# Two four-image tiles become eight one-image units in a diffusion and deformable-convolution kernel

## The chip, the cores and the metric

The kernel runs on one core of a Trainium2 chip. The metric is the device time of one execution in microseconds. The core has a matrix engine (PE, with its weight loads shown apart as PEld), a vector engine (DVE), an activation engine (ACT), GpSimd (POOL) and a sync engine that issues DMAs (SP). Each works through its own instruction list in order and waits on semaphores.

## The reference

`x` is `(8, 32, 32, 64)` in float32 (image, row, column, channel). Two residual layers, each behind a group normalization with groups of two channels, act on it. The first is five steps of a diffusion whose coefficients come from gradients and two depthwise 3x3 convolutions; the second is a deformable 3x3 convolution that samples nine displaced points per pixel bilinearly.

```python
g, g1 = relu(bn(dwconv(h, wg))), relu(bn(dwconv(h, wg1)))
gy, gx = sobel(h)
Dx, Dy = 1 / (gy*gy/4 + 1), 1 / (gx*gx/4 + 1)
...
for _ in range(5):
    prev = h
    h = D * (c0*h0 - 2*E*h + cm_x*roll(h, 1, 2) + cp_x*roll(h, -1, 2)
             + cm_y*roll(h, 1, 3) + cp_y*roll(h, -1, 3)) + D * 0.4 * fsrc
    h0 = prev
...
o1, o2, m = split(conv3x3(x, w_offset) + b_offset)   # 9 + 9 + 9 channels
sampled = bilinear(x, base_y + o1, base_x + o2) * sigmoid(m)   # 9 taps, 64 channels
out = einsum('bkcp,fck->bfp', sampled, filt)
```

## The kernel before

128 partitions hold the 32 rows of four images. There are two tiles (`TILES`) of four images; a tile's free dimension is 32 columns by 64 channels, 2048 numbers per partition (`WC`). Each tile goes through normalization, gradients, depthwise convolution, coefficients, 20 diffusion chunks of 512 numbers (`pde 0` to `pde 19`), the second normalization and the offsets. Then its 32 image columns are sampled one by one.

The sampling of a column works so. SP has written the normalized tile into a table in HBM, in which one entry of 1 KB holds the four corner pixels of a bilinear sample. POOL issues nine gathers per column (L378), one for each tap, each of 128 rows by 1 KB. DVE multiplies the gathered corners by their weights (L748), adds them in two steps (L755, L761), PE transposes the sums in five 128x128 pieces (L1056), ACT copies them to SBUF (L921), and PE multiplies with the filter (L1064, five products with 64 columns). A group of four columns is added to `x1` (L730) and stored (L356). `pixels` has room for four columns.

The order of the work on DVE, ACT and PE is one list written out by hand (`SCHEDULE`, turned into `ORDER`): tile 0 up to its first column, then tile 1's pieces with tile 0's columns between them, then tile 1's columns alone. In the second and third part the table of tile 1 is written and POOL goes on from tile 0's 288 gathers to tile 1's 288. SP first issues the loads, then eight DMAs that clear the table (L338), then per tile eight that fill it (L351).

In the diffusion PE sums five products per chunk by multiplying them with the identity (L1037); DVE forms the products (L576, L580, L586), both operands in SBUF, and adds the kept rest (L597). In the profile one call of `matmul` on float32 is two MATMUL records; one `transpose` is one record.

## Time and profile before

| | |
|---|---|
| time, median of 3 runs | 1076.55 us (1072.9 to 1078.05) |
| the profiled execution | 1075.92 us, its span 1074.0 us |
| busy: PE, PEld | 612.7 us (57%), 399.3 us (37%) |
| busy: DVE, ACT | 673.2 us (63%), 214.5 us (20%) |
| busy: POOL | 628.6 us (59%), of it 626.3 us in 576 gathers |
| first and last gather start | 251.7 and 1058.0 us |
| mean granted clock of PE | 0.727 of 2.4 GHz |

Busy time is what the instructions of an engine cover. Two matmuls in a row overlap in the records, so what one costs in a stream is the distance between starts. DMA-issuing time of SP is not counted as busy.

### The profile page before, as it was taken

The numbers are of one execution on the slowest core, as the hardware profiler recorded it, in microseconds if no ns is written. First come the engines' busy times: TensorE is split into PE (matmuls) and PEld (weight loads), VectorE is DVE, ScalarE is ACT, GpSimd is POOL, SyncE is SP. The second block draws the span as 40 slices with busy tenths as digits, with TensorE's granted clock in tenths as the row PEclk, the third lists the DMA queues.
The fourth block names the chain that finished last, engine by engine and source line by source line (L and its number), as shares of the span: only waits on it lengthen the run. The fifth ranks groups of instructions, "written<-read, shape, count | busy, mean of one in ns | idle before, by whom it ended". The sixth has DMA issues, their size and how long they took to land.

```text
span 1074.0 us, 7428 instructions
## 1 busy us (share of the span) xinstructions
PE 612.7 (57%) x2314; PEld 399.3 (37%) x2314; DVE 673.2 (63%) x685; ACT 214.5 (20%) x577; POOL 628.6 (59%) x588
## 2 busy tenths in 40 slices
PE   1987999468985678958843667523222322322233
PEld 1773434123775244434323433323222322322233
DVE  6799999843788676858887446543344334334433
ACT  2721000022523223133213411200000000000000
POOL 0000000004888777877787777777777777777773
PEclk9998999779987878987975686655555555555555
DMA  6431000054222233233222583333333333333331
GB/s 217 132 120 43 0 0 1 0 110 111 84 74 74 79 93 93 77 87 95 85 83 88 133 254 105 93 106 103 107 99 105 107 97 107 101 107 98 106 107 56
DMA packets 58144, 100.35 MB, mean 93 GB/s; under 512 B 10168, under 2 KB 39040, under 8 KB 57856
## 3 DMA queue, kind: packets, MB, share of 16 engines
q0 software_dynamic: 27648, 75.53, 23.8%
q1 hardware_dynamic: 30464, 24.42, 8.4%
q8 instruction: 17, 0.28, 0.1%
q14 instruction: 15, 0.12, 0.0%
HBM read 79.13 MB, written 20.78 MB: 93 GB/s over the span
## 4 chain that ended last, share of the span: by engine, by line
POOL 58%; issue 20%; DVE 12%; PE 5%; ACT 2%; DMA 2%; SPq 1%; POOLq 0%; DVEq 0%
POOL pixels L378 57%; PE acc L1037 3%; DVE rsum L434 2%; SPq L351 1%; DVE shared L586 1%; DVE shared L576 1%; DMA table<-scratch 1%; DVE h_pad L597 1%; DVE shared L556 1%; DVE shared L580 1%; PE acc L959 1%; DMA x<-x_in 0%; DVE scratch L430 0%; DVE scratch L415 0%; PE acc L1005 0%
## 5 line engine op out<-in xcount | busy, mean ns | idle before, releaser
L378 POOL DMA_INDIRECT pixels<-table,index_now x576 | 626.3, 1087 | 180.2 <-issue 172.4
L748 DVE TENSOR_TENSOR pixels<-pixels,side 128x2304 f32<-128x2304 f32 (+1 forms) x64 | 148.2, 2315 | 260.8 <-DMA pixels<-table,index_now 260.4
L1056 PE MATMUL side<-const,sums 128*128 128x128 f32 x320 | 74.1, 388 | 352.7 <-DVE sums L761 324.4
L1037 PE MATMUL acc<-shared,const 128*128 128x512 f32 x400 | 196.1, 635 | 22.7 <-DVE shared L576 22.7
L1056 PEld LDWEIGHTS side<-const,sums 128*128 128x128 f32 x320 | 53.3, 199 | 369.4 <-issue 239.3
L370 POOL COPY index_now<-index 128x72 uint32 x8 | 2.1, 260 | 250.0 <-DMA table<-scratch 250.0
L921 ACT ACTIVATE sampled_T<-side 128x384 f32<-128x384 f32 (+1 forms) x128 | 49.7, 433 | 403.3 <-PE side L1056 403.2
L1064 PEld LDWEIGHTS side<-filt,sampled_T 128*128 128x128 f32 x640 | 126.3, 296 | 0.0
L1064 PE MATMUL side<-filt,sampled_T 128*128 128x64 f32 x640 | 125.8, 373 | 0.0
L1037 PEld LDWEIGHTS acc<-shared,const 128*128 128x128 f32 x400 | 77.8, 202 | 128.0 <-issue 108.3
L755 DVE TENSOR_TENSOR pixels<-pixels 128x1152 f32<-128x1152 f32 x64 | 86.9, 1358 | 7.4 <-ACT pixels L910 5.4
L910 ACT ACTIVATE pixels<-pixels,corner_w 128x64 f32<-128x64 f32 x228 | 56.5, 334 | 135.6 <-DMA pixels<-table,index_now 135.6
L586 DVE TENSOR_TENSOR shared<-arrays,h_pad 128x1024 f32<-128x1024 f32 x40 | 48.8, 1220 | 7.4 <-PE acc L1037 7.3
L580 DVE TENSOR_TENSOR shared<-arrays,h_pad 128x1024 f32<-128x1024 f32 x40 | 48.7, 1219 | 5.5 <-PE acc L1037 5.5
L761 DVE TENSOR_TENSOR sums<-pixels 128x576 f32<-128x576 f32 x64 | 48.5, 758 | 4.9 <-PE side L1056 0.5
L959 PE MATMUL acc<-conv_w,shared 128*128 128x256 f32 x128 | 39.5, 391 | 4.5 <-DVE h_pad L509 4.5
L576 DVE TENSOR_TENSOR shared<-arrays,h_pad 128x512 f32<-128x512 f32 x40 | 27.5, 688 | 18.4 <-ACT h_pad L800 18.4
L935 PE MATMUL acc<-rsum,const 128*128 128x64 f32 x16 | 4.9, 403 | 54.8 <-DVE rsum L434 54.0
L597 DVE TENSOR_TENSOR h_pad<-acc,shared 128x512 f32<-128x512 f32 x40 | 27.4, 685 | 2.1 <-PE acc L1037 2.1
L556 DVE TENSOR_TENSOR shared<-arrays,h_pad 128x512 f32<-128x512 f32 x40 | 27.6, 690 | 0.9
L1035 PE MATMUL acc<-arrays,const 128*128 128x512 f32 x50 | 25.5, 593 | 0.0
L935 PEld LDWEIGHTS acc<-rsum,const 128*128 128x128 f32 x16 | 3.6, 281 | 57.2 <-DVE rsum L434 55.6
(158 smaller groups left out, 744.0 us busy)
## 6 DMA issues: line engine op xcount, KB each, us to landing
table<-corner_w SPq DMA_DIRECT2D x8, 1225.0 KB
pixels<-table,index_now POOLq DMA_INDIRECT x576, 2.8
table<-scratch SPq DMA_DIRECT2D x16, 528.0 KB, 10.4
x<-x_in SPq DMA_DIRECT2D x2, 1024.0 KB, 7.2
out_dram<-x SPq DMA_DIRECT2D x16, 128.0 KB, 1.9
const<-const_in SPq DMA_DIRECT2D x1, 641.0 KB, 6.0
xn_next<-bn_in SPq DMA_DIRECT2D x1, 384.0 KB, 7.1
off_w<-offw_in SPq DMA_DIRECT2D x1, 288.0 KB, 7.1
```

The lines of the kernel that those rows point to most:

```text
L378: pool.indirect_dma_start(out=pixels[:, w % COLS, k, :], out_offset=None, in_=table, in_offset=bass.IndirectOffsetOnAxis(ap=index_now[:, o ...
L580: dve.tensor_tensor(two(wc(prod[:, prod_slot(n, 1), :]), wc(prod[:, prod_slot(n, 2), :])), two(coef(2), coef("mid")), two(moved(0, -1), mo ...
L586: dve.tensor_tensor(two(wc(prod[:, prod_slot(n, 3), :]), wc(prod[:, prod_slot(n, 4), :])), two(coef(3), coef(0)), two(moved(-1, 0), moved( ...
L748: dve.tensor_tensor(quads[:, 0:cells, :], quads[:, 0:cells, :], weights[:, 0:cells].unsqueeze(2).to_broadcast([P, cells, C]), ALU.mult)\
L755: dve.tensor_tensor(px[:, :, 0:2 * C], px[:, :, 0:2 * C], px[:, :, 2 * C:4 * C], ALU.add)\
L761: dve.tensor_tensor(sums[:, j % 2, 0:K2 * C].rearrange("p (k c) -> p k c", c=C), px[:, :, 0:C], px[:, :, C:2 * C], ALU.add).then_inc(s_sum ...
L910: ins = act.activation(cell, cell, ACT.Copy, scale=corner_w[:, 0, w, 4 * k + q:4 * k + q + 1])
L921: act.activation(sampled_T[:, j % 2, a * P:b * P], turned[:, r, 0:(b - a) * P], ACT.Copy)\
L959: ins = pe.matmul(dst, turned_pair(dh, pair), w3[:, 0:4 * C], start=dh == 0, stop=False)
L1037: pe.matmul(bank(t, "pde", i), eye, prod[:, prod_slot(n, j), :], start=j == 0, stop=j == PRODS - 1)\
L1056: ins = pe.transpose(turned[:, r, (i - a) * P:(i - a + 1) * P], sums[:, j % 2, i * P:(i + 1) * P], eye)
L1064: ins = pe.matmul(out[:, j * C:(j + 1) * C], sampled_T[:, j % 2, k * P:(k + 1) * P], filt[:, k, :], start=k == 0, stop=k == TAP_PAIRS - 1)
```

## The change

A unit is now one image: its 32 columns are split into four sides of 8 columns, and partition `side * 32 + row` holds one side of a row. `WC` becomes 512, one PSUM bank. There are eight units, each with 8 columns per partition to sample, so 64 columns and 576 gathers in all, as before.

- The list of pieces per unit is `BESIDE`: eight parts, and part `w` of unit u+1 stands ahead of column `w` of unit u. The prediction calls part `w` with the column behind it slot `w`. Unit 0's parts stand alone at the start.
- The diffusion's arrays, of 512 numbers per partition, lie in PSUM banks 0 to 3; DVE's large operations then take one operand at least from PSUM. The neighbours across sides come by products with `prev` and `next`, so a step has nine products: four of 448 to 504 columns, one of 512, two of 64 and two of 8. DVE no longer adds the rest, it seeds the target bank.
- Column: DVE only multiplies, into `weighted`. PE adds the four corners while it transposes: for each of five pieces four transposing products accumulate (20 in all, "flips"). Then the filter as before.
- `pixels` has room for seven columns, and POOL takes its indices from `index` without a copy.
- The loads are 42 DMAs instead of 8, ahead of the eight that clear the table, and the table is filled per unit by eight DMAs of 32 by 8 or 9 entries' halves.
- The depthwise convolution is 13 products per half unit (one of 512, six of 384 and six of 128 columns), the offsets are 19 of 27 to 216 columns, the gradients 13.

```diff
-PARTS = ((0, 3), (3, TAP_PAIRS))
...
+PARTS = ((0, 4), (4, TAP_PAIRS))
+NB = 7
...
-SCHEDULE = [
-    (0, "sum1, centre1, square1, deviation1, scale1, turn, rows, sobel, denominator, conv 0, gates 0, conv 1, "
...
+BESIDE = ("sum1 centre1 square1 scale1 turn", "grad den conv-0 log seed", "dterms conv-1 da own coef",
+          "pde-0 pde-1", "pde-2 pde-3", "pde-4 final sum2 centre2", "square2 scale2 halo turn2", "off samp")
+ORDER = [(0, piece) for part in BESIDE for piece in part.split()]
+for u in range(UNITS):
+    for w in range(WS):
+        if u + 1 < UNITS:
+            ORDER += [(u + 1, piece) for piece in BESIDE[w].split()]
+        ORDER.append((u, f"column-{w}"))
...
+            def write_table(u):
+                sp.wait_ge(*emptied(u, "halo"))
+                for s in range(SIDES):
+
+                    count = WS + 1 if s == 0 else WS
+                    side = xn2[s * H:(s + 1) * H, WS + 1 - count:WS + 1, :]
+                    pairs = bass.AP(tensor=side.tensor, offset=side.offset,
+                                    ap=[list(side.ap[0]), [C, count], [1, 2 * C]])
+                    at = LO + (s + 1) * WS - count
+                    for k in range(2):
+                        sp.dma_start(table_y[u, LO - k:LO - k + H, at:at + count,
+                                             k * 2 * C:(k + 1) * 2 * C], pairs).then_inc(s_table, 16)
...
+            for u in range(UNITS):
+                pool.wait_ge(s_table, 16 * TABLE_DMAS * (u + 1))
+                pool.wait_ge(s_index, u + 1)
+                for w in range(WS):
+                    col = u * WS + w
+                    if col >= NB:
+                        pool.wait_ge(s_weighted, col - NB + 1)
+                    for k in range(K2):
+                        at = col * K2 + k
+                        pool.indirect_dma_start(
+                            out=pixels[:, col % NB, k, :], out_offset=None, in_=table,
+                            in_offset=bass.IndirectOffsetOnAxis(ap=index[:, at:at + 1], axis=0),
+                        ).then_inc(s_pixels[col % NB], 16)
 
...
+            def step(u, m):
...
+                seq(dve.tensor_tensor(target(m), c0[:, :], source(m) if m == 0 else target(m), ALU.mult))
+                dve.tensor_tensor(target(m), target(m), force[:, :], ALU.add).then_inc(s_seeded, 1)
...
+                for dirs in (slice(1, 5, 2), slice(2, 5, 2)):
+                    dve.tensor_tensor(prod[:, dirs, :], coef[:, dirs, :],
+                                      source(m).unsqueeze(1).to_broadcast([P, 2, WC]), ALU.mult).then_inc(s_prod, 1)
+                dve.tensor_tensor(prod[:, 0, :], coef[:, 0, :], source(m), ALU.mult).then_inc(s_prod, 1)
...
-                dve.tensor_tensor(px[:, :, 0:2 * C], px[:, :, 0:2 * C], px[:, :, 2 * C:4 * C], ALU.add)\
...
-                dve.tensor_tensor(sums[:, j % 2, 0:K2 * C].rearrange("p (k c) -> p k c", c=C),
-                                  px[:, :, 0:C], px[:, :, C:2 * C], ALU.add).then_inc(s_sums, 1)
...
+                dve.tensor_tensor(weighted[:, col % 2, :, 0:K2, :].rearrange("p q k c -> p k q c"),
+                                  pixels[:, col % NB, :, :].rearrange("p k (q c) -> p k q c", c=C),
+                                  weights.unsqueeze(3).to_broadcast([P, K2, 4, C]), ALU.mult).then_inc(s_weighted, 1)
+                if j == 1 and big:
+                    add_group(big - 1)
...
+            def step(u, m):
+                n = u * STEPS + m
+                T = wc(target(m))
+                left, below, right, up = (wc(prod[:, i, :]) for i in range(1, 5))
+
+                pe.wait_ge(s_seeded, n + 1)
+                pe.wait_ge(s_prod, 3 * n + 1)
+                mm(T[:, 1:WS, :], eye, left[:, 0:WS - 1, :])
+                mm(T[:, 0, :], M["prev"], left[:, WS - 1, :])
+                mm(T[:, 0:WS - 1, :], eye, right[:, 1:WS, :])
+                mm(T[:, WS - 1, :], M["next"], right[:, 0, :])
+                pe.wait_ge(s_prod, 3 * n + 2)
+                mm(T[:, :, 1:C], eye, below[:, :, 0:C - 1])
+                mm(T[:, :, 0:1], eye, below[:, :, C - 1:C])
+                mm(T[:, :, 0:C - 1], eye, up[:, :, 1:C])
+                mm(T[:, :, C - 1:C], eye, up[:, :, 0:1])
+                pe.wait_ge(s_prod, 3 * n + 3)
+                mm(T, eye, wc(prod[:, 0, :]), stop=True).then_inc(s_h, 1)
...
-                    ins = pe.transpose(turned[:, r, (i - a) * P:(i - a + 1) * P],
-                                       sums[:, j % 2, i * P:(i + 1) * P], eye)
...
+            def column(col):
+                pe.wait_ge(s_weighted, col + 1)
+                for r, (a, b) in enumerate(PARTS):
+                    if col:
+                        pe.wait_ge(s_sT, (col - 1) * len(PARTS) + r + 1)
+                    for k in range(a, b):
+                        for q in range(4):
+                            ins = flip(turned[:, r, (k - a) * P:(k - a + 1) * P],
+                                       weighted[:, col % 2, q, 2 * k:2 * k + 2, :].rearrange("p k c -> p (k c)"),
+                                       eye, q == 0, q == 3)
+                    ins.then_inc(s_part, 1)
+                if col:
+                    filtered(col - 1)
```

How the two programs stand on PE. Before, the place is where tile 1's fifth diffusion chunk stands between two columns of tile 0 (`sums` are a column's sums, `shared` a chunk's products):

```order
L1056 MATMUL side<-const,sums 128x128 [waits sampled_T_ready,column_summed]
L1056 MATMUL side<-const,sums 128x128 x2
L1056 MATMUL side<-const,sums 128x128 [waits sampled_T_ready]
L1056 MATMUL side<-const,sums 128x128
L1064 MATMUL side<-filt,sampled_T 128x64 [waits sampled_T_ready]
L1064 MATMUL side<-filt,sampled_T 128x64 x4
L1037 MATMUL acc<-shared,const 128x512 [waits product_ready,bank_emptied_by_dve]
L1037 MATMUL acc<-shared,const 128x512 [waits product_ready] x3
L1035 MATMUL acc<-arrays,const 128x512 [waits product_ready]
L1037 MATMUL acc<-shared,const 128x512
```

Of the change, PE where unit 1's diffusion steps 1 and 2 stand around column 3 of unit 0 (`weighted` are a column's weighted corners, `prod` a step's products):

```order
L693 MATMUL banks<-prod,const 128x512 [waits products_ready]
L696 MATMUL banks<-const,weighted 128x128 [waits sampled_T_ready,weighted]
L696 MATMUL banks<-const,weighted 128x128 x15
L696 MATMUL banks<-const,weighted 128x128 [waits sampled_T_ready]
L696 MATMUL banks<-const,weighted 128x128 x3
L693 MATMUL banks<-filt,sampled_T 128x64 [waits sampled_T_ready]
L693 MATMUL banks<-filt,sampled_T 128x64 x4
L693 MATMUL banks<-prod,const 128x448 [waits products_ready,target_seeded]
L693 MATMUL banks<-prod,const 128x64
L693 MATMUL banks<-prod,const 128x448
L693 MATMUL banks<-prod,const 128x64
L693 MATMUL banks<-prod,const 128x8x63 [waits products_ready]
```

A column is now 20 transposing products and 5 of the filter where 5 and 5 stood, and a whole step of the next unit waits behind it. On ACT, the list of slot 1 in the change (squares of the gradients, then the gates of the convolution, then logarithm and exponential; `sampled_T` is column 1's copy):

```order
L607 ACTIVATE banks<-banks 128x512 [waits bank_full]
L608 ACTIVATE b_more<-banks,scalars 128x512 [waits scalar_step]
L610 ACTIVATE banks<-banks 128x512 [waits bank_full]
L653 ACTIVATE gates<-banks 128x512 [waits bank_full]
L657 ACTIVATE log_t<-t_arr,scalars 128x512 [waits t_ready]
L659 ACT_TABLE_LOAD
L659 ACTIVATE banks<-log_t 128x512 [waits scalar_step]
L592 ACT_TABLE_LOAD
L592 ACTIVATE unused<-scalars 128x1
L631 ACTIVATE sampled_T<-banks 128x512 [waits part_turned]
```

Before, the same engine had nothing between the squares and the logarithm:

```order
L870 ACTIVATE arrays<-arrays 128x2048 [waits gradient_ready] x2
L873 ACT_TABLE_LOAD
L873 ACTIVATE arrays<-arrays,den_const 128x2048 [waits denominator_ready]
L874 ACT_TABLE_LOAD
L874 ACTIVATE arrays<-arrays 128x2048 [waits scalar_step]
```

The logarithm has moved behind the gates of the first half of the convolution, which wait for 13 products of PE.

## Rows read from the trace of the kernel before

**Rows 1.** The page: the last chain's shares by engine; a gather's us to landing.

```profile
POOL 58%; issue 20%; DVE 12%; PE 5%; ACT 2%; DMA 2%; SPq 1%; POOLq 0%; DVEq 0%
...
pixels<-table,index_now POOLq DMA_INDIRECT x576, 2.8
```

**Rows 2.** Timeline, start and duration in us, columns alone, 850 to 856 us.

```profile
849.79 2.56 DVE L748 TENSOR_TENSOR pixels<-pixels,side 128x2304 f32<-128x2304 f32 x1 [6.81 <-DMA pixels<-table,index_now]
850.71 0.94 POOL L378 DMA_INDIRECT pixels<-table,index_now  x1 [0.30 <-issue]
852.38 1.36 DVE L755 TENSOR_TENSOR pixels<-pixels 128x1152 f32<-128x1152 f32 x1
853.20 1.35 POOL L378 DMA_INDIRECT pixels<-table,index_now  x1 [0.30 <-issue]
```

**Rows 3.** Timeline of PE at the high clock: chunk sums, transposes, filter.

```profile
353.37 1.02 PE L1021 MATMUL acc<-scratch,const 128*128 128x512 f32 x2
...
491.27 0.71 PE L1056 MATMUL side<-const,sums 128*128 128x128 f32 x5
491.82 1.23 PE L1064 MATMUL side<-filt,sampled_T 128*128 128x64 f32 x10
```

**Rows 4.** Timeline of PE after idle stretches (in brackets, us).

```profile
402.07 1.33 PE L1056 MATMUL side<-const,sums 128*128 128x128 f32 x5 [5.68 <-DVE sums L761]
403.19 2.24 PE L1064 MATMUL side<-filt,sampled_T 128*128 128x64 f32 x10
405.22 5.87 PE L1037 MATMUL acc<-shared,const 128*128 128x512 f32 x8
...
428.74 5.58 PE L1037 MATMUL acc<-shared,const 128*128 128x512 f32 x8 [3.07 <-DVE shared L576]
...
483.96 5.76 PE L1037 MATMUL acc<-shared,const 128*128 128x512 f32 x8 [9.73 <-DVE shared L576]
```

**Rows 5.** Groups by line, shapes apart: busy us, mean ns of one.

```profile
L748 DVE TENSOR_TENSOR pixels<-pixels,side 128x2304 f32<-128x2304 f32 x45 | 114.9, 2554 | 244.7 <-DMA pixels<-table,index_now 244.5
L580 DVE TENSOR_TENSOR shared<-arrays,h_pad 128x1024 f32<-128x1024 f32 x40 | 48.7, 1219 | 5.5 <-PE acc L1037 5.5
L597 DVE TENSOR_TENSOR h_pad<-acc,shared 128x512 f32<-128x512 f32 x40 | 27.4, 685 | 2.1 <-PE acc L1037 2.1
L861 ACT ACTIVATE arrays<-acc 128x512 f32<-128x512 f32 x16 | 9.0, 632 | 1.7 <-PE acc L1005 1.6
L874 ACT ACT_TABLE_LOAD x2 | 2.6, 1283 | 0.0
L403 DVE TENSOR_TENSOR gtmp<-grstd 128x32 f32<-128x32 f32 x4 | 0.8, 192 | 0.1
```

**Rows 6.** Timeline of SP at the start and at the first filling.

```profile
0.75 0.40 SPq L326 DMA_DIRECT2D x<-x_in  x1
...
4.88 73.60 SPq L338 DMA_DIRECT2D table<-corner_w  x8
224.51 18.09 SPq L351 DMA_DIRECT2D table<-scratch  x8
```

**Rows 7.** Windows: busy us (count) of PE, PEld, DVE, ACT, POOL; PEclk, DMA share, GB/s.

```profile
93.00:94.00 1.00, 1.00 (x4) 0.52 (x3) 0.96 (x2) 0.00 (x0) 0.00 (x0) 1.00 0.03 9
```

**Rows 8.** First copy; all gathers (ns min/median/max, first and last start); DVE's last operation.

```profile
250.42 0.24 POOL L370 COPY index_now<-index 128x72 uint32 x1 [249.96 <-DMA table<-scratch]
...
L378 POOL DMA_INDIRECT pixels<-table,index_now x576: 942/946/3023, 251.7 to 1058.0; - x192
...
1071.14 0.42 DVE L730 TENSOR_TENSOR x<-side,x 128x256 f32<-128x256 f32 x1 [5.58 <-PE side L1064]
```

**Rows 9.** The 16 transposes at 224 us, and windows as in Rows 7.

```profile
224.48 3.68 PE L943 MATMUL acc<-const,scratch 128*128 128x128 f32 x16 [4.41 <-DVE scratch L430]
...
226.00:228.00 2.00, 2.00 (x11) 1.75 (x9) 1.91 (x1) 2.00 (x6) 0.00 (x0) 0.50 0.96 176
...
230.00:232.00 2.00, 2.00 (x7) 0.70 (x6) 0.00 (x0) 1.78 (x4) 0.00 (x0) 1.00 0.98 176
```

More of the change, by code:

```diff
@@ new lines, in build_program @@
+        pos = sb("pos", [P, WS * 2 * K2])
+        low = sb("low", [P, WS * 2 * K2])
+        above = sb("above", [P, WS * 2 * K2])
+        pos_int = sb("pos_int", [P, WS * 2 * K2], i32)
+        mask = sb("mask", [P, WS * K2])
+        bottom = sb("bottom", [P, WS * K2])
+        top = sb("top", [P, WS * K2])
+        corner_w = sb("corner_w", [P, 2, WS, K2 * 4])
+        index = sb("index", [P, UNITS * WS * K2], u32)
+        pixels = sb("pixels", [P, NB, K2, ENTRY])
+        weighted = sb("weighted", [P, 2, 4, 2 * TAP_PAIRS, C])
@@ L309, in prod_slot, with bank, full @@
[L309 to L321 removed]
+        def bank(u, what, q=0):
+            return banks[:, PLAN[AT[u, what, q]][3], :]
+        def full(u, what, q=0):
+            return AT[u, what, q] + 1
@@ L780, in _ @@
+            for u, part in ORDER:
+                name, _, i = part.partition("-")
+                piece(u, name, int(i or 0))
+            add_group(UNITS * GROUPS_U - 1)
         @block.scalar
@@ new lines, in norm_root, with turned_main @@
+            def norm_root(u, which):
+                act.wait_ge(*emptied(u, f"square{which}"))
+                act.activation(grstd[:, :], gvar[:, :], ACT.Sqrt, bias=gn_eps).then_inc(s_sd, 1)
+            def turned_main(u, what):
+                act.wait_ge(s_full, full(u, what, 0))
+                for dh in (1, 0, 2):
+                    ins = act.activation(*shifted_rows(rows(xT[:, dh, 0:PAIRS * P]), rows(bank(u, what, 0)), dh),
+                                         ACT.Copy)
+                ins.then_inc(s_act, 1)
@@ L927, in _ @@
+            act.wait_ge(s_setup, 1)
+            prepare(ACT.Sqrt)
+            for u, part in ORDER:
+                name, _, i = part.partition("-")
+                piece(u, name, int(i or 0))
         @block.tensor
         def _(pe):
[L929 to L935 removed]
@@ L1049, in turn_part, with wait_bank_empty @@
-            def turn_part(first, col, j, r):
-                if not (first and j == 0):
-                    pe.wait_ge(s_sT, col * len(PARTS) + (r + 1 - len(PARTS)))
-                a, b = PARTS[r]
-                for i in range(a, b):
-                    ins = pe.transpose(turned[:, r, (i - a) * P:(i - a + 1) * P],
-                                       sums[:, j % 2, i * P:(i + 1) * P], eye)
-                ins.then_inc(s_part, 1)
-            def filtered(col, j, out):
+            def wait_bank_empty(u, what, q=0):
+                n = AT[u, what, q]
+                before = [f for f in PLAN[:n] if f[3] == PLAN[n][3]]
+                if before and before[-1][4]:
+                    pe.wait_ge(*emptied(*before[-1][:3]))
@@ new lines, in mm, with flip, group_sum @@
+            def mm(dst, lhsT, rhs, start=False, stop=False):
+                return pe.matmul(dst, lhsT, rhs, start=start, stop=stop, skip_group_check=True)
+            def flip(dst, data, moved, start=True, stop=True):
+                return pe.matmul(dst, data, moved, start=start, stop=stop, is_transpose=True, skip_group_check=True)
+            def group_sum(u, what, src):
+                wait_bank_empty(u, what)
+                for i in range(WC // P):
+                    ins = mm(bank(u, what)[:, 0:P], M["ones"], src[:, i * P:(i + 1) * P], i == 0, i == WC // P - 1)
+                ins.then_inc(s_full, 1)
@@ new lines, in spread @@
+            def spread(dst, first, w3, slots, dh, width, cols, stop):
+                for k, slot in enumerate(slots):
+                    at = {LEFT: -2, RIGHT: WS}.get(slot, 2 * slot) - 1
+                    a, b = max(at, first), min(at + 4, first + cols)
+                    ins = mm(dst[:, (a - first) * width:(b - first) * width], xT[:, dh, slot * P:(slot + 1) * P],
+                             w3[:, (a - at) * width:(b - at) * width], stop=stop and k == len(slots) - 1)
+                return ins
```

1326 lines of the change are left out of this document (556 added, 770 removed).

## The prediction

> **What bounds the kernel now.** The first view is the chain that ended last: POOL's gathers and the gaps between them hold 78% of it [rows 1]. The timeline shows why. In the columns of the last stage a gather takes 0.94 to 0.95 us and the next one comes 0.30 us later, so 1.25 us each, or 11.25 us for a column's nine. It is longer when DVE has both operands in SBUF: beside L755 it took 1.35 us, while beside L748, whose weights lie in PSUM, it stayed at 0.94 [rows 2]. From the first gather to the last, 251.7 to 1058.0 us, are 575 steps of 1.40 us on average. So before falls into a head of 250 us without a gather, which ends when the table is filled, 807 us of gathers, and 15 us of tail after the last gather's end at 1059.0 [rows 8]. DVE, PE and ACT hide behind POOL in all but the head and the tail.
>
> **What the change takes away.** The gathers stay 576. With no large two-SBUF operation left they should cost 720 us instead of 807. The head shrinks: one image's chain is a quarter of the former. What ends it then is the clearing of the table: its eight DMAs were first issued at 4.88 us [rows 6] and moved data until 94 us [rows 7], 89 us. Eight loads were issued in 4.1 us, 0.52 each [rows 6]; the change issues 42, so clearing begins at about 22 us and ends at 106 to 111, less a few us since no loads compete; I take 107. Filling was eight DMAs, 224.5 to 250.4 us, for four images [rows 6, 8]; for one image a quarter of the bytes is 6.5 us, and with landing I take 8. First gather: 115 us. If POOL stayed the bound, the end would be 115 + 8 x 90 + 17 = 852 us, the tail being longer by the added transposes. I don't expect that, because of what follows.
>
> **What the change adds: a chain per unit.** Unit u+1's gathers need its indices, which come out of slot 7 beside unit u. Every engine goes through the slots in order. PE reaches slot w+1's pieces only after column w's 20 flips and 5 filter products, which wait for DVE's multiplication; DVE's pieces wait for PE; and DVE's next multiplication stands behind them. So the slots' latencies add up, and POOL's seven buffers don't help, since it runs out of indices, not of room. I call the sum P, the time from one unit's indices to the next's. POOL needs 90 us for a unit; everything of P above that is POOL idle.
>
> Prices at the high clock. Two records of 512 columns take 1.02 us, 0.43 from start to start plus 0.16 at the end; a float32 product is two records, so 0.86 for 512 columns, in proportion down to 0.21 for 128 columns or less, which is the pace of the filter's ten records (1.23 us). Five transposes took 0.55 up to the next group's start, 0.11 each [rows 3]. At the low clock all of that doubles: five transposes 1.12, ten records 2.03, 512 columns 0.86 per record [rows 4]. DVE: 0.69 for 512 numbers per partition, 1.22 for 1024, 2.56 for the multiplication, 0.19 for the small ones; ACT 0.63 for 512, 1.28 for a table load [rows 5]. A handover is about 0.05. These operations have the old shapes or sizes between them, except PSUM as the destination of large DVE operations; L597 reads PSUM at the SBUF pace, and I price writing the same (a slower bound: ten per cent on some 15 operations, 1 us a unit).
>
> A column on PE is thus 20 x 0.11 + 10 x 0.107 = 3.3 us. The slots, from one multiplication's end to the next, at the high clock:
>
> - Slot 0: column 3.3; sums of x on PE 1.0; reduce and centre 1.0; square 0.7; sums 1.1; reduce, root and four small steps 1.5, scaling 0.7; six flips 0.9; three copies 0.9; weights and multiplication 2.9. 14.0 us.
> - Slot 1: column 3.3; gradients 5.6 (13 products, 2,304 wide columns and eight narrow products); half a convolution 6.1 (3,584 columns); gates 0.7; logarithm 0.7, table load 1.3, exponential 0.7; five DVE operations 3.6; multiplication 2.6. 24.6 us. ACT's list puts the gates before the logarithm, so the convolution is on the path.
> - Slot 2: column 3.3; half a convolution 6.1; gates 0.7; d_gates 1.3; coefficients 3.0, beside PE's own sums (4.0); one more 0.7; multiplication 2.6. 17.7 us.
> - Slots 3 to 5: five steps. PE needs 4.9 us a step (1.9 after the first products, 2.1 after the second, 0.85 for the last), DVE 1.2 until PE can start, and a column goes in front of every second step. Slot 3: column 3.3, step to 8.4, DVE's products for the next to 11.4, multiplication to 14.0. Slot 4: PE finishes step 1 at 0.7, the column at 3.9, step 2 at 9.0; DVE's products to 12.1, weights and multiplication to 15.0. Slot 5: column to 3.5, last step to 8.6, scale 0.8, shift on PE 1.1, add 0.8, sums 1.1, reduce and centre 1.0, multiplication 2.6: 16.0 us.
> - Slot 6: column 3.3; sums 1.1; reduce to scaling 2.2; flips 1.1; copies 0.9; multiplication 2.6. 11.2 us.
> - Slot 7: column 3.3; offsets 4.4 (19 products at the floor of 0.21, one a little more); eight small steps to the indices 2.4; seven more 2.1; multiplication 2.6. 14.8 us.
>
> Sum: 127.3 us, of it 82 us PE work. That is 37 above POOL's 90 already.
>
> The low clock comes on top. PE idles for 3.4 to 10 us ahead of the columns that begin slots 0, 1, 2, 6 and 7, since each of those slots ends in DVE work. In the trace, PE after 5.68 us of idling ran the column slow and 4 us more; after 9.73 us the eight records took 5.76 instead of 3.6; after 3.07 us still 5.58 [rows 4]. Five columns at 6.5 instead of 3.3 are 16 us; the short groups of slots 0 and 6 in slow stretches up to 4 more; now and then the clock holds. I take 17, so P = 144. The steps keep PE nearly busy and should run at the high clock.
>
> On the flips the Trainium skill speaks against the change: the page TensorE: Matmul & The Clock Gate, section PE-mode transpose, says that transposes don't count as activity, so that the full clock doesn't come. In the trace 16 transposes alone, begun at the low clock (0.50 from 226 to 228 us), were followed by 1.00 from 230 us, after 1.2 us of two products [rows 9]. So I don't take the rule; what it would make is the third rival.
>
> **Sum.** First multiplication ends at 115 + 11.25 + 2.8 + 2.56 = 131.6. Unit 1's indices follow after P less slot 0 (19 in the mixed state) and less the 4.7 us of slot 7 behind them: 120.3, at 252. Six more periods: 864, at 1116. The last unit's gathers 90, at 1206. Tail: landing 2.8, multiplication 2.6, 20 slow flips 4.5, two filter groups 4.2, add 0.5, store 2.4: 17. Span 1223; in general 215 + 7P. The profiled execution stood 1.9 us above its span and 0.6 below the median, so 1225 us.
>
> **The rivals.**
> 1. The high clock holds throughout: P = 127.3 with slot 0 at 14, 220 + 891 = 1111, with the 1.9 above the span 1113. Rows 4 speak against it, chance 0.11.
> 2. Faster: PE overlaps more than its records show (narrow products below 0.21, weight loads of the flips taken early while DVE still multiplies other pieces), and the slots shrink. It decides at P = 122.7, where 215 + 7P is the old span; below that each us is worth 7, down to 852 with POOL as the bound. It needs 4.6 us less than the high-clock sum and no slow stretch. The streams of rows 3 are dense already. Chance 0.07 faster, and 0.02 for what falls within 0.5% (a measurement of this kernel can't tell less).
> 3. The flips leave the clock low, or the steps fall to it: eight columns at 6.5 (+26) and 4 us of slow work behind each (+16): P = 169, 1400 us. For it: columns alone never reached the high clock in the last stage of before. Against: rows 9. Chance 0.10.
> 4. The forecast, P between 135 and 156, 1160 to 1310 us: chance 0.70.
>
> The range takes in the forecast and rival 1: 1105 to 1310 holds 0.81. Faster 0.07, same 0.02, slower 0.91.
>
> **What would show it.** First gather near 115 us, released by a table DMA. Gathers at 0.95 us nearly throughout, POOL busy near 550 us. Before seven of the gathers, each the first of a unit, POOL idle 40 to 65 us, released by DVE's index. Columns of slots 0 and 1 at a clock of 0.50, steps at 1.00; PE busy over 60%. Slot 1 the longest, with about 10 us between the end of PE's convolution and the next flips. Wrong if the units follow each other at less than 125 us, if POOL has no such idle stretches, or if the step group of nine products takes much under 4.9 us or PE starts it before the column ahead is done.

## The result and the profile after

The changed kernel takes 1198.2 us, median of four runs (1197.5 to 1199.4), beside 1076.9 for the kernel before: a ratio of 1.1135, 95% interval [1.1105, 1.1165]. The forecast was 1225 with a range of 1105 to 1310. The profiled execution has a span of 1197.5 us at a mean granted clock of 0.83.

The page of the changed kernel (busy us and share of the span; PEclk in 40 slices; the last chain by engine):

```profile
PE 811.0 (68%) x4112; PEld 626.7 (52%) x4112; DVE 528.7 (44%) x772; ACT 209.7 (18%) x403; POOL 547.8 (46%) x589
...
PEclk8995779877898689977899778986899778996667
...
PE 56%; DVE 19%; SPq 7%; POOL 6%; issue 5%; DMA 3%; ACT 3%; POOLq 0%; DVEq 0%
```

The chain that was POOL's to 58% [rows 1] is now PE's and DVE's to 75%, and PEclk shows a wave that repeats with the units. POOL's part is seen in its gathers (duration ns min/median/max, first and last start) and in the timeline at the first gather of all and at the first gather of a later unit:

```profile
L342 POOL DMA_INDIRECT pixels<-table,index x576: 940/946/1087, 116.1 to 1182.4; - x192
...
116.05 1.09 POOL L342 DMA_INDIRECT pixels<-table,index  x1 [112.33 <-DMA table<-xn]
...
673.76 0.95 POOL L342 DMA_INDIRECT pixels<-table,index  x1 [50.27 <-issue]
```

There are the same 576 gathers as in rows 8, the longest 1.09 us where it was 3.02; the first starts at 116 instead of 252 us. But POOL stands for 50 us ahead of each of the last six units (48.3 ahead of unit 1). The first gathers of units 1 to 7 start at 254.1, 393.9, 533.8, 673.8, 813.7, 953.7 and 1093.6 us: a unit follows the other after 139.9 us, and of these the gathers use 89.7.

The next view is DVE's timeline, the multiplication alone, one period from slot 7's to slot 7's. From one row's end to the next one's is a slot:

```profile
675.09 2.55 DVE L528 TENSOR_TENSOR weighted<-pixels,banks 128x2304 f32<-128x2304 f32 x1
692.51 2.56 DVE L528 TENSOR_TENSOR weighted<-pixels,banks 128x2304 f32<-128x2304 f32 x1
719.17 2.55 DVE L528 TENSOR_TENSOR weighted<-pixels,banks 128x2304 f32<-128x2304 f32 x1
739.31 2.55 DVE L528 TENSOR_TENSOR weighted<-pixels,banks 128x2304 f32<-128x2304 f32 x1
753.28 2.55 DVE L528 TENSOR_TENSOR weighted<-pixels,banks 128x2304 f32<-128x2304 f32 x1
768.46 2.55 DVE L528 TENSOR_TENSOR weighted<-pixels,banks 128x2304 f32<-128x2304 f32 x1
784.89 2.55 DVE L528 TENSOR_TENSOR weighted<-pixels,banks 128x2304 f32<-128x2304 f32 x1
798.12 2.54 DVE L528 TENSOR_TENSOR weighted<-pixels,banks 128x2304 f32<-128x2304 f32 x1
815.04 2.55 DVE L528 TENSOR_TENSOR weighted<-pixels,banks 128x2304 f32<-128x2304 f32 x1
```

Slots 0 to 7 are 17.4, 26.7, 20.1, 14.0, 15.2, 16.4, 13.2 and 16.9 us. At the full clock 14.0, 24.6, 17.7, 14.0, 15.0, 16.0, 11.2 and 14.8 were forecast. PE's timeline in slot 1 and the windows of slots 0 to 3 (busy us and count of PE, PEld, DVE, ACT, POOL; PEclk, DMA share, GB/s) tell which slots are longer, and why:

```profile
695.12 4.39 PE L696 MATMUL banks<-const,weighted 128*128 128x128 f32 x20 [3.77 <-DVE weighted L528]
699.35 1.23 PE L693 MATMUL banks<-filt,sampled_T 128*128 128x64 f32 x10
700.41 5.82 PE L693 MATMUL banks<-xn,const 128*128 128x448 f32 x26
...
706.98 5.37 PE L693 MATMUL banks<-conv_w,xT 128*128 128x128 f32 x24
721.78 3.46 PE L696 MATMUL banks<-const,weighted 128*128 128x128 f32 x15 [9.43 <-DVE weighted L528]
...
741.91 2.40 PE L696 MATMUL banks<-const,weighted 128*128 128x128 f32 x20 [2.75 <-DVE weighted L528]
...
675.00:692.50 17.50, 9.26 (x52) 8.48 (x52) 6.79 (x15) 4.86 (x9) 13.24 (x14) 0.70 0.35 106
692.50:719.20 26.70, 17.23 (x82) 13.01 (x82) 6.74 (x8) 7.30 (x12) 20.29 (x22) 0.82 0.36 104
719.20:739.30 20.10, 16.60 (x76) 12.57 (x76) 8.12 (x13) 3.16 (x7) 15.23 (x17) 0.82 0.39 113
739.30:753.30 14.00, 9.98 (x54) 6.96 (x55) 10.99 (x13) 1.49 (x5) 10.65 (x12) 1.00 0.37 107
```

After 3.77 us of idling the 20 flips take 4.39 us, in slot 3 at a clock of 1.00 they take 2.40. The ten records of the filter behind the slow flips already run at the full clock's 1.23 us. Slots 3 to 5 stay at 1.00 and are within 0.4 us of the forecast; the others are longer by 2.0 to 3.4 us. The convolution ends at 712.35, and PE waits 9.43 us for DVE.

### The profile page after: what moved, and what is told of

The parts are those of the page before. It is cut to its first block, busy times and chain, and to the rows that moved or that the text cites. A ratio compares the mean times of both kernels' runs of the same rounds, so it can differ in the third digit from the quotient of the medians.

```text
span 1197.5 us, 10571 instructions
## 1 busy us (share of the span) xinstructions
PE 811.0 (68%) x4112; PEld 626.7 (52%) x4112; DVE 528.7 (44%) x772; ACT 209.7 (18%) x403; POOL 547.8 (46%) x589
## 4 chain that ended last, share of the span: by engine, by line
PE 56%; DVE 19%; SPq 7%; POOL 6%; issue 5%; DMA 3%; ACT 3%; POOLq 0%; DVEq 0%
PE banks L693 38%; PE banks L696 18%; DVE weighted L528 9%; POOL pixels L342 6%; SPq L288 5%; DMA table<-corner_w 2%; DVE prod L462 1%; SPq L264 1%; DVE xn L377 1%; ACT L659 1%; ACT gates L653 1%; DVE xT L410 1%; SPq L303 1%; DMA table<-xn 1%; DMA pixels<-table,index 0%
## 5 line engine op out<-in xcount | busy, mean ns | idle before, releaser
L342 POOL DMA_INDIRECT pixels<-table,index x576 | 544.6, 946 | 635.0 <-issue 522.3
L696 PE MATMUL banks<-const,weighted 128*128 128x128 f32 x1280 | 240.6, 370 | 263.9 <-DVE weighted L528 263.9
L696 PEld LDWEIGHTS banks<-const,weighted 128*128 128x128 f32 x1280 | 222.4, 197 | 281.3 <-DVE weighted L528 262.1
L693 PE MATMUL banks<-prod,const 128*128 128x448 f32 (+2 forms) x720 | 208.6, 441 | 28.9 <-DVE prod L462 28.9
L528 DVE TENSOR_TENSOR weighted<-pixels,banks 128x2304 f32<-128x2304 f32 x64 | 163.2, 2551 | 78.8 <-DMA pixels<-table,index 60.6
L693 PEld LDWEIGHTS banks<-prod,const 128*128 128x128 f32 x720 | 109.5, 192 | 111.1 <-issue 111.1
L462 DVE TENSOR_TENSOR prod<-coef,banks 128x1024 f32<-128x1024 f32 x80 | 93.9, 1215 | 59.9 <-PE banks L693 59.9
L693 PE MATMUL banks<-conv_w,xT 128*128 128x384 f32 (+1 forms) x384 | 88.1, 387 | 0.0
L693 PEld LDWEIGHTS banks<-filt,sampled_T 128*128 128x128 f32 x640 | 85.4, 210 | 0.0
L693 PE MATMUL banks<-filt,sampled_T 128*128 128x64 f32 x640 | 84.0, 282 | 0.0
```

Of the source, the lines that this page charges most:

```text
L342: pool.indirect_dma_start(out=pixels[:, col % NB, k, :], out_offset=None, in_=table, in_offset=bass.IndirectOffsetOnAxis(ap=index[:, at:at ...
L462: dve.tensor_tensor(prod[:, dirs, :], coef[:, dirs, :], source(m).unsqueeze(1).to_broadcast([P, 2, WC]), ALU.mult).then_inc(s_prod, 1)
L528: dve.tensor_tensor(weighted[:, col % 2, :, 0:K2, :].rearrange("p q k c -> p k q c"), pixels[:, col % NB, :, :].rearrange("p k (q c) -> p ...
L693: return pe.matmul(dst, lhsT, rhs, start=start, stop=stop, skip_group_check=True)
L696: return pe.matmul(dst, data, moved, start=start, stop=stop, is_transpose=True, skip_group_check=True)
```

## Experiments

The first theory was that of the prediction: **lockstep**, so that a period is the sum of the slots' latencies, with a share that is only the clock. Its rivals: gathers that pace the columns, waits that are not the clock, flips that lie beside other work. All times are medians of four runs. Where only the period changes, the formula 215 + 7P of the prediction is held against the span.

**Gathers left out.** Five of nine taps are gathered, the rest stay zero.

```diff
+TAKEN = 5
...
-                    for k in range(K2):
+                    for k in range(TAKEN):
...
-                dve.wait_ge(s_pixels[col % NB], (col // NB + 1) * 16 * K2)
+                dve.wait_ge(s_pixels[col % NB], (col // NB + 1) * 16 * TAKEN)
```

> The changed kernel, with five of nine taps gathered: four ninths of GpSimd's DMA issues are left out, and the pixels of taps 5 to 8 are the zeros that GpSimd writes once at the start (so the output lacks these taps). All of VectorE's, TensorE's and ScalarE's work stays. Theory A, that the gathers (90 us a unit, in a period of 139.9) are hidden behind the lockstep of TensorE and VectorE: the period stays at 139 to 140.5 us, and only the first column and the last unit gain, about 40 to 45 us together: 1150 to 1160 us. Theory B, that the gathers pace the columns: the period falls by 20 us or more, and the time to below 1050 us.

1153.4 us, ratio 1.0717 [1.0695, 1.0740] to before. DVE's multiplications, two at the same slot of units one apart:

```profile
513.22 2.54 DVE L532 TENSOR_TENSOR weighted<-pixels,banks 128x2304 f32<-128x2304 f32 x1
...
653.17 2.54 DVE L532 TENSOR_TENSOR weighted<-pixels,banks 128x2304 f32<-128x2304 f32 x1
```

139.95 us from one to the other, the old period to 0.1 us, with 228 us of POOL's work gone. The 45 us gained lie in the first column and in the last unit, which alone wait for gathers. Theory A holds; the gathers don't pace the units.

**The clock held by added matmuls.**

```diff
+FILL = (12, 36, 8, 0, 0, 12, 12, 26)
...
+                if col and col < (UNITS - 1) * WS:
+                    pe.wait_ge(s_sT, col * len(PARTS))
+                    for _ in range(FILL[col % WS]):
+                        mm(turned[:, 0, 0:P], eye, eye, True, True)
                 pe.wait_ge(s_weighted, col + 1)
```

> The changed kernel, with matmuls that compute nothing put ahead of the flips, where TensorE would wait for VectorE's products: in seven units 12, 36, 8, 0, 0, 12, 12 and 26 of them in slots 0 to 7 (fp32, 128 columns each; they write the piece of the turned banks that the flips then overwrite, and no result changes). They do no work that was missing; all that they can change is TensorE's clock in the matmuls that come behind them. Theory A, that slots 0, 1, 6 and 7 are longer than on the full clock because TensorE has fallen to 1.2 GHz beside waits, and that the unit period of 139.9 us holds about 12.7 us of this: the granted clock of the span goes from 0.83 to 0.9 or more, the period to 128 to 132 us and the time to 1115 to 1145 us. Theory B, that the surcharge is not the clock but waits between engines (semaphores, VectorE's own durations): the period stays at 139 to 141 us, or is longer by what the added matmuls delay, 1195 to 1230 us.

1139.5 us, ratio 1.0577 [1.0551, 1.0603]: 59 us less with 113 us more of PE work (923.9 busy), at a clock of 0.916. PE's timeline over slots 0 and 1 of this kernel:

```profile
654.73 3.83 PE L694 MATMUL banks<-const 128*128 128x128 f32 x22
658.39 2.35 PE L697 MATMUL banks<-const,weighted 128*128 128x128 f32 x20
...
673.41 8.20 PE L694 MATMUL banks<-const 128*128 128x128 f32 x72
683.01 2.18 PE L697 MATMUL banks<-const,weighted 128*128 128x128 f32 x18 [1.39 <-DVE weighted L529]
```

The flips behind the added work take 2.35 instead of 4.39 us. The slots from the same kind of rows are 14.9, 24.7, 17.9, 14.0, 15.2, 16.4, 12.4 and 16.0, in sum 131.4 us; 215 + 7P is 1135, the span 1138.0. Slots 0 to 5 are now within 0.9 us of the sum for the full clock; so 8.5 us of the period went with the clock. In slots 6, 7 and 0 it was still 0.86 to 0.89, so part of the 4.1 us that are left above 127.3 may be clock too; no run separates this. Theory A.

**One part of slot 1 moved off the chain.** The first half of the convolution goes behind the logarithm and the seed.

```diff
-BESIDE = ("sum1 centre1 square1 scale1 turn", "grad den conv-0 log seed", "dterms conv-1 da own coef",
+BESIDE = ("sum1 centre1 square1 scale1 turn", "grad den log seed conv-0", "dterms conv-1 da own coef",
...
-         "conv-0": [("conv", 0, 2, "act", "conv-0")],
+         "conv-0": [("conv", 0, 3, "act", "conv-0")],
```

> The changed kernel, with one move: the first half of the depthwise convolution stands behind the logarithm and the seed in slot 1, not ahead of them, and writes bank 3 in place of bank 2 (correct output). It takes 13 matmuls and a ScalarE copy out of the chain from the gradients to the diffusion's coefficients, and lays them beside VectorE's work on the seed. Theory A, lockstep: a unit's period is the sum of what each slot takes in order, so slot 1 (26.65 us) loses 5 to 6 us and the period goes from 139.9 to about 134.5 us: 1155 to 1170 us. Theory B, that the slots share one bound (the total of TensorE's work, or the gathers, that a shorter slot doesn't shorten): the period stays within 1 us and the time within 1190 to 1205 us.

1171.6 us, ratio 1.0879 [1.0855, 1.0903]. (The convolution no longer writes the whole of bank 2 ahead of the diffusion, and this changes what the steps accumulate there: against what was expected, the output lacks part of these sums, while the operations and their sizes are all there. The woven order below has the same move, starts the four flips of that bank only once and keeps the sums in full.) The multiplications that end slots 0 to 3, and the flips of slot 3:

```profile
673.86 2.55 DVE L528 TENSOR_TENSOR weighted<-pixels,banks 128x2304 f32<-128x2304 f32 x1
695.29 2.55 DVE L528 TENSOR_TENSOR weighted<-pixels,banks 128x2304 f32<-128x2304 f32 x1
714.70 2.54 DVE L528 TENSOR_TENSOR weighted<-pixels,banks 128x2304 f32<-128x2304 f32 x1
730.32 2.54 DVE L528 TENSOR_TENSOR weighted<-pixels,banks 128x2304 f32<-128x2304 f32 x1
...
717.29 3.70 PE L696 MATMUL banks<-const,weighted 128*128 128x128 f32 x20 [2.75 <-DVE weighted L528]
```

Slot 1 is 21.4 us, 5.2 less, as expected for it. But slot 3 is 15.6 instead of 14.0 and slot 6 14.8 instead of 13.2, though nothing in them was changed: of 5.2 us the period gives back 2.2 (137.0 us). The time, 1172, lies just above the range expected. The clock accounts for both slots: in slot 3 it is 0.89 instead of 1.00, and the flips that took 2.40 us take 3.70; in slot 6 it is 0.62 instead of 0.87. So a slot's length hangs on what PE did in the ones before.

**Three of four flips left out.**

```diff
-                        for q in range(4):
+                        for q in range(1):
...
-                                       eye, q == 0, q == 3)
+                                       eye, True, True)
```

> The changed kernel, with one flip of each piece in place of four that accumulate: 15 of the 20 flips of a column are left out (three of four corners are left out of the output), VectorE's product over all four corners stays. Theory A, that the flips lie in the chain of every slot: the 15 flips cost what the profile shows for them in each slot, 1.7 to 3 us by the clock, so the period falls by 14 to 16 us to 124 to 126 us and the time to 1080 to 1100 us, near the kernel before. Theory B, that TensorE has slack beside a column (VectorE's products set the pace): the period falls by less than 5 us, time over 1160 us.

1194.1 us, ratio 1.1092 [1.1069, 1.1115], 4 us below the changed kernel. Theory A fails in its size; B has the number right, but not the reason, as the rows show. The period is 139.95 us, as in the changed kernel. The groups of PE by line of the changed kernel, and under them those of this one (busy us, mean ns, idle before and releaser):

```profile
L696 PE MATMUL banks<-const,weighted 128*128 128x128 f32 x1280 | 240.6, 370 | 263.9 <-DVE weighted L528 263.9
...
L693 PE MATMUL banks<-filt,sampled_T 128*128 128x64 f32 x640 | 84.0, 282 | 0.0
```

```profile
L693 PE MATMUL banks<-filt,sampled_T 128*128 128x64 f32 x640 | 123.1, 367 | 0.0
...
L696 PE MATMUL banks<-const,weighted 128*128 128x128 f32 x320 | 72.4, 380 | 282.6 <-DVE weighted L528 282.6
```

The flips' busy time falls by 168 us, but PE's by only 31 (811.0 to 780.3): the filter alone, the same 640 records, takes 39 us more. The mean clock is 0.715 instead of 0.83. The window of slot 3 and PE's rows there, and ahead of them the filter of slot 0, say it most plainly:

```profile
674.20 2.23 PE L693 MATMUL banks<-filt,sampled_T 128*128 128x64 f32 x10
...
733.70:749.80 16.10, 11.60 (x39) 6.97 (x40) 10.99 (x13) 1.49 (x5) 12.13 (x14) 0.79 0.35 103
...
736.30 0.77 PE L696 MATMUL banks<-const,weighted 128*128 128x128 f32 x5 [2.75 <-DVE weighted L528]
...
738.85 8.01 PE L693 MATMUL banks<-prod,const 128*128 128x448 f32 x18 [0.50 <-DVE prod L462]
```

The 18 records of the diffusion step, 5.16 us in the changed kernel, take 8.01 here. Slot 3 is 16.1 us instead of 14.0, though 1.6 us of flips are gone from it; slot 7 is 18.7 instead of 16.9, with its offset products at 7.72 us instead of 4.10; slots 4 and 5 are 1.6 and 1.3 us shorter, near the flips' own price. In slot 0, which stands at a clock of 0.50, the filter takes 2.23 us behind five flips, where it took 1.30 behind twenty. Two slots lose 3.9 us in all and the others gain 3.9; that these come to the same, and the period stays to 0.05 us, is chance. So my theory had to be changed: in this kernel the flips hold the clock up for the work behind them, and they are paid for by it.

**The corner part undone.** VectorE adds, five flips a column.

```diff
+                here = weighted[:, col % 2, :, 0:K2, :]
+                dve.wait_ge(s_multiplied, col + 1)
+                seq(dve.tensor_tensor(here[:, 0:2], here[:, 0:2], here[:, 2:4], ALU.add))
+                dve.tensor_tensor(here[:, 0], here[:, 0], here[:, 1], ALU.add).then_inc(s_weighted, 1)
...
-                        for q in range(4):
+                        for q in range(1):
```

> The changed kernel with its corner part undone: VectorE adds the four corners of a column in two steps, and TensorE flips five pieces once in place of five times four (correct output). Leaving the 15 flips out had moved the time by 4 us only (1198 to 1194), with the granted clock down from 0.83 to 0.715 and the matmuls that stayed slower by about as much as the flips had cost. Theory A, lockstep with a clock that falls with TensorE's work: the two adds (1152 and 576 elements for each partition, about 1.3 and 0.7 us by VectorE's other rows, 2.2 with their handovers) come on top of the leaner flips, whose saving the clock takes back; the period goes from 139.9 to about 156 to 160 us and the time to 1315 to 1350 us, with a clock of 0.7 or less. Theory B, that flips and adds can be priced by themselves (1.9 us of flips saved against 2.2 us of adds in each slot): within 15 us of the changed kernel, 1190 to 1215 us.

This kernel and two more below first ran on a chip where the kernel before took 1177.5 us in place of 1076 to 1077, and there it took 1789 us. What such chips do to these kernels is told at the end; nothing about the theories follows from those runs. So it ran again:

> The kernel of the run with the adds back once more, unchanged, since the chip of that run had slowed the kernel before too (1177 us in place of 1077): the changed kernel, with the corners added on VectorE in two steps and five pieces of a column flipped once each (correct output). Without the adds this kernel took 1194 us, with a period of 139.95 us and a clock of 0.715. Theory A, lockstep with a clock that falls with TensorE's work: the adds, about 2.2 us in each slot, come on top, and the period goes to 156 to 160 us, the time to 1315 to 1350 us. Theory B, each part priced by itself: 1190 to 1215 us.

1316.2 us, ratio 1.2232 [1.2212, 1.2253], with before at 1076.0 and a clock of 0.71. DVE's timeline of a column:

```profile
667.53 2.55 DVE L529 TENSOR_TENSOR weighted<-pixels,banks 128x2304 f32<-128x2304 f32 x1
670.11 1.36 DVE L534 TENSOR_TENSOR weighted<-weighted 128x1152 f32<-128x1152 f32 x1
671.50 0.76 DVE L535 TENSOR_TENSOR weighted<-weighted 128x576 f32<-128x576 f32 x1
```

The adds lengthen a column by 2.17 us and eight of them by 17.4; the period is 157.4 us (599.02 to 756.41 for the same slot), 17.4 above that of the run before with the same flips, and 215 + 7P is 1317. Theory A, to a tenth of a us a unit, though single slots grow by 1.2 to 2.6 us. The accumulating flips in place of the adds are thus worth 118 us in this order: nearly all of the adds' price, 122, since the flips' own is 4.

**The columns woven into the chain.** A column becomes two pieces, the product (W) and flips, copies and filter (F). The last column of a unit (marked -) goes beside the norm of the unit two behind. The first half of the convolution stands behind the logarithm, as in the run on slot 1. (What the expectation of the second run below calls the kernel of four units is the kernel before, with its two tiles.)

```diff
+CHAIN = ("sum1 centre1 W7- square1 F7- scale1 turn grad den W0 log seed conv-0 F0 dterms conv-1 "
+         "W1 da own coef F1 pde-0 W2 pde-1 F2 W3 pde-2 F3 pde-3 W4 pde-4 F4 final sum2 centre2 W5 "
+         "square2 F5 scale2 halo turn2 W6 off F6 samp")
...
-                    ins = flip(bank(u, what, 0)[:, i * P:(i + 1) * P], src[:, i * P:(i + 1) * P], eye)
+                    ins = flip(bank(u, what, 0)[:, i * P:(i + 1) * P], src[:, i * P:(i + 1) * P], eye, i == 0)
```

> The changed kernel with another order: a column is no longer one step at a slot's end. Its product on VectorE and its flips, copies and filter on TensorE and ScalarE are two pieces, and they stand at different places of the next unit's chain: the product where TensorE works (ahead of the logarithm, beside the second convolution, between diffusion steps), the flips where VectorE works; the last column of a unit goes beside the norm of the unit two behind. The first convolution stands behind the logarithm, as in the run before, and the four flips that fill its neighbour bank start it only once (correct output). All the work stays. Theory A, that the period of 139.9 us is the sum of handovers in a fixed order, most of it 264 us of TensorE waiting for the products and the low clock that comes with it: the period falls to 101 to 115 us, bounded below by the gathers' 90, and the time to 930 to 1035 us, faster than the kernel before. Theory B, that eight units of one image each cost their chains whatever the order (each chain has as many handovers as that of a unit of two images): the period stays over 125 us and the time over 1090 us.

1482.1 us on that chip. And again:

> The woven order once more, unchanged. In the run before, the kernel of four units itself took 1177 us in place of 1077, and TensorE stood for 1 to 2.6 us between single flips while gathers were issued, with nothing in the trace to wait for. Theory A, that this is a trait of the chip or of its state at that time and not of the order: with the kernel before back at 1077 us this kernel takes 930 to 1035 us (period 101 to 115 us), without such stands. Theory B, that gathers beside woven columns starve TensorE's instruction supply on any chip: over 1300 us again.

928.0 us (926.1 to 932.2), ratio 0.863 [0.8603, 0.8656] to before, and about 0.775 to the changed kernel's 1198 (not run side by side): the version that beats both. Its page, the groups of PE and DVE that were the wait, and POOL at two units' first gathers:

```profile
PE 753.8 (81%) x4112; PEld 577.3 (62%) x4112; DVE 526.9 (57%) x772; ACT 206.2 (22%) x403; POOL 548.0 (59%) x589
...
PEclk9998589999999799999999799989998899986766
...
L705 PE MATMUL banks<-const,weighted 128*128 128x128 f32 x1280 | 185.3, 310 | 55.4 <-DVE weighted L537 55.4
...
720.16 0.94 POOL L351 DMA_INDIRECT pixels<-table,index  x1 [11.54 <-issue]
...
820.28 0.94 POOL L351 DMA_INDIRECT pixels<-table,index  x1 [10.39 <-issue]
```

The same 4,112 records of PE, the same flips: PE waits 55 us for products instead of 264, the clock is 0.91, and the flips cost 185 us instead of 241. The period is 100 to 103 us, and POOL stands for 10 to 13 us a unit instead of 50. Theory B, that eight chains cost what they cost, is out: it was the order within them. Of the 270 us, the move of the convolution was worth 27 by itself; the rest, 244, comes with the woven columns, and no run weaves them without that move.

**What stayed open.** Two kernels never met a chip on which before was at 1077: three flips left out with the added matmuls (1633.9 and 1635.7 us, before at 1178 and 1150), and the woven order with VectorE's adds (1570.8 and 1560.6, before at 1174 and 1157). Their edits are those above, put together, but for 8 added matmuls in slots 3 and 4 also.

> The changed kernel with one flip of each piece in place of four (three of four corners left out of the output) and with the added matmuls that compute nothing ahead of the flips, 12, 36, 8, 8, 8, 12, 12 and 26 in slots 0 to 7, where TensorE waits for the product. Theory A, that leaving the flips out saved nothing because the clock fell: with the clock held (0.88 or more) the flips' time at the full clock comes off the run that had only the added matmuls (1139.5 us): 15 flips at 0.11 to 0.12 us, 1.7 us in each of 64 columns, about 105 us: 1030 to 1060 us. Theory B, that the flips lie beside other work and cost nothing anyhow: 1125 to 1145 us, as with the added matmuls alone.

> The kernel with one corner's flips and the added matmuls once more, unchanged, since the chip of the first try had slowed the kernel before too: one flip of each piece in place of four (three corners left out of the output), and 12, 36, 8, 8, 8, 12, 12 and 26 matmuls that compute nothing ahead of the flips in slots 0 to 7. Theory A, that leaving the flips out had saved nothing because the clock fell: with the clock held (0.88 or more) the 15 flips of a column, 1.7 us at the full clock, come off the period of 131.4 us of the run with the added matmuls alone: 117 to 120 us, and 1030 to 1060 us in all. Theory B, that the flips lie beside other work: period 130 us or more, 1125 to 1145 us.

> The woven order with the adds of the corners back on VectorE, and five pieces of a column flipped once each (correct output). In the woven order the period is 100.1 us, TensorE is busy for 81% of the span, VectorE for 57%, and the gathers need 89.7 us. Theory A, that TensorE's total is what bounds the woven period, so that the flips now have a price: 15 flips, 1.7 us at the full clock, leave each of the 64 columns, and the 2.2 us of adds lie where VectorE waits: the period falls to 91 to 97 us, and the time to 865 to 905 us. Theory B, that the chain of handovers between the engines still sets the period, and VectorE's adds stand in it and take the flips' share of the clock with them: 2.2 us for each of eight columns, a period of 108 to 118 us and 985 to 1060 us.

> The woven order with the adds back on VectorE once more, unchanged, since the chip of the first try had slowed the kernel before too (correct output). Woven with accumulating flips it is 928 us, with a period of 100.1 us. Theory A, that TensorE's total bounds the woven period: 15 flips of a column, 1.7 us at the full clock, are gone and the adds lie where VectorE waits: a period of 91 to 97 us, 865 to 905 us in all. Theory B, that the chain of handovers still sets the period and the adds stand in it: 108 to 118 us, 985 to 1060 us in all.

All four are outside of both theories, and decide between none. That the flips have a price of their own once the clock is held is argued from the 2.35 us that 20 of them take at the full clock, and was not measured; nor was it measured whether the adds would win in the woven order.

## Why the prediction was right

**POOL.** The first gather was put at 115 us and came at 116.1, held back by the table's DMA as said; the gathers at 0.95 us, POOL busy for 548. Its idling was put at 40 to 65 us before seven gathers, and was 48 to 50; the profile names no releaser ("issue"), where I had said that it would name DVE's index.

**The sum P.** 127.3 us at the full clock and 17 for the low one, 144; measured 139.9. The slots at the full clock are the stronger part: three to five were within 0.4 us, and with the clock held the whole was 131.4, where slots 6 and 7 are 1.2 us longer each and make up most of the 4.1 us between them. **The term that was mis-sized is the surcharge**: 12.7 us in the changed kernel, of which 8.5 is clock that added matmuls could take away. Its 16 us for five slow columns, 3.2 each, took the price of a column at the low clock from rows 4, where ten slow filter records (2.03 us) follow five flips. Behind twenty flips the filter is already fast. From the first flip to the end of the filter the columns at the starts of slots 0, 1, 2, 6 and 7 take 5.5, 5.3, 5.6, 5.0 and 5.4 us where 6.5 stood, 10 us over 3.3 in all instead of 16. The forecast was 252 + 6 x 144 + 90 + 17 = 1223; measured are 254.1 for unit 1's first gather, 6 x 139.9, 89.8 from the last unit's first gather to the end of its last (1182.4 and 0.94), and 14.2 of tail, together the span of 1197.5. The six periods are 24.6 of the 25.5 us between them, and 2.1 and 2.8 of the head and the tail nearly cancel. The longest slot was slot 1, and PE's wait in it 9.43 us where "about 10" stood.

**The rivals.** The full clock throughout (1113) lies 85 us below what came, and the added matmuls, at 0.916, brought 1139.5. Rows 4 were rightly read against it: without added work PE falls back. The rival that flips leave the clock low, P = 169, was wrong by its reason and not only by its size: without 15 of them the clock falls from 0.83 to 0.715, and the filter's records from 282 to 367 ns. The Trainium skill (TensorE: Matmul & The Clock Gate, PE-mode transpose) says that transposes don't count as activity; for these float32 flips this case's runs speak against it, as rows 9 had. The prediction reads rows 9 more weakly than it could: the window from 228 to 230 us has a mean clock of 0.81, which puts the rise near 228.8, and the first of the two products starts only at 228.99.

**What the working did not see.** It prices each operation and adds; by that the 15 flips were a cost of 1.65 us in each of eight slots, 13 a unit. Left out, they saved 4 us in the whole kernel. A price at a fixed clock holds only while the rest keeps PE as busy as it was, and the sum for a kernel without them would have been 13 us a unit too low. The forecast escaped this since it left the flips in.

## What to carry to other kernels

When engines go through hand-ordered pieces in lockstep, add the slots' latencies and ask which piece could stand elsewhere: the time here came not from fewer operations but from putting a column's product where TensorE works and its flips where VectorE works, with the convolution moved off the chain (1198 to 928 us, of which that move alone gave 27). Before taking work off TensorE beside its waits, read the granted clock there; work that looks like the cost may be what keeps the rest at full speed.

## What the runs showed of the hardware

**The clock follows the work, flips too.** 15 of 20 flips less in each column: clock 0.83 to 0.715 and 4 us saved. 1,460 added matmul records more: 0.916 and 59 us saved. What was left out or added shows in the records that come behind it: the filter's at 367 ns instead of 282, the flips at 2.35 us instead of 4.39.

**On some chips TensorE stands while gathers are issued.** On the chips where the kernel before took 1150 to 1178 us, the woven kernel took 1482 us. Its timeline on PE there, in the first unit's columns, two windows (with gathers and without), and PEld's largest wait (us in total, times, longest); under them the same wait of the same kernel at 928 us:

```profile
137.70 0.27 PE L705 MATMUL banks<-const,weighted 128*128 128x128 f32 x1 [1.82 <-issue]
139.13 0.37 PE L705 MATMUL banks<-const,weighted 128*128 128x128 f32 x1 [1.16 <-issue]
...
148.22 0.37 PE L705 MATMUL banks<-const,weighted 128*128 128x128 f32 x1 [2.42 <-issue]
151.02 0.37 PE L705 MATMUL banks<-const,weighted 128*128 128x128 f32 x1 [2.43 <-issue]
...
290.00:368.00 78.00, 25.38 (x92) 16.60 (x91) 7.54 (x18) 5.82 (x11) 59.10 (x63) 0.60 0.35 103
...
395.00:467.00 72.00, 63.18 (x340) 47.62 (x341) 46.22 (x65) 9.48 (x22) 0.00 (x0) 0.91 0.09 18
...
PEld banks L702 <- issue: 644.5, 708, 33.4
```

```profile
PEld banks L702 <- issue: 158.3, 525, 3.7
```

The flips, whose product was ready at 131.3 us, come 1.4 to 2.8 us apart, and the stands of up to 33 us have no releaser in the trace. POOL goes on with its gathers at 1.25 us meanwhile. In 78 us with gathers PE runs 92 records, in 72 us without them 340. Gathers alone don't make it, though: from 383 to 394 us PE is busy throughout beside nine of them. It costs before 7 to 9%, the kernel with the adds 36% (1316 to 1789) and the woven one 60%. What these chips share, and whether the supply of instructions is what is late, the trace doesn't tell, and I didn't try it. A time of such a chip is not held against another's here; the kernel before, run beside each, is what showed it.
